# A second product with the scores in the quarters of a unit that have no experts' work, in a four-layer kernel on one Trainium2 core

## The reference, cut to what matters

```
for layer in 0, 1, 2, 3:
    xn = layernorm(x)
    x = x + attention(layer, xn) + feed_forward(layer, xn)
```

```
scores = q @ k.T * scale          # 512 x 512
p = softmax(scores)
o = p @ v
```

## Time and profile before

| what | value |
|---|---|
| median of 3 runs | 2046.42 us (2044.97 to 2046.79) |
| the profiled execution's own time | 2032.71 us |
| its span | 2030.9 us |
| its mean TensorE clock | 0.781 |
| TensorE busy | 1417.9 us (70%) |
| TensorE weight loads | 636.1 us (31%) |
| VectorE busy | 1310.7 us (65%) |
| ScalarE busy | 971.2 us (48%) |
| GpSimd busy | 290.0 us (14%) |

### The profile page before, as it was taken

One profiled execution on the slowest core, in us unless ns is written; L12 is line 12 of the kernel. 1 busy time (PEld: TensorE's weight loads), 2 busy tenths in 40 slices (PEclk: granted clock), 3 DMA queues, 4 the chain that ended last, 5 costly groups with the idle time before them and its releaser, 6 DMA issues.

```text
span 2030.9 us, 22370 instructions
## 1 busy us (share of the span) xinstructions
PE 1417.9 (70%) x6401; PEld 636.1 (31%) x6402; DVE 1310.7 (65%) x4041; ACT 971.2 (48%) x2237; POOL 290.0 (14%) x383
## 2 busy tenths in 40 slices
PE   6889799862244203641888998886877499899983
PEld 2445444431112101210355554221222133343331
DVE  5979889878888864761565665674565355455451
ACT  3889888834434441110455554443443244444441
POOL 0201010010000000266010011532013201000023
PEclk7989999985555555555998898676776799899995
DMA  3010001005000000221412232221102230111111
GB/s 109 24 47 25 40 30 37 1 11 191 1 0 1 0 1 23 72 77 44 107 57 75 75 102 62 62 39 50 36 28 49 84 113 21 25 56 44 40 31 49
DMA packets 151439, 98.41 MB, mean 48 GB/s; under 512 B 73328, under 2 KB 136117, under 8 KB 151265
## 3 DMA queue, kind: packets, MB, share of 16 engines
q1 hardware_dynamic: 145175, 84.40, 14.2%
q0 software_dynamic: 6144, 12.60, 2.2%
HBM read 60.83 MB, written 35.73 MB: 48 GB/s over the span
## 4 chain that ended last, share of the span: by engine, by line
PE 46%; DVE 30%; issue 8%; ACT 6%; another core or an unknown queue 6%; SPq 2%; DMA 2%; DVEq 0%
PE PS L465 38%; DVE RA L1560 5%; PE PS L461 4%; DVE RA L1562 4%; DVE nmx L1310 3%; DVE RA L1114 3%; DVE RA L1117 3%; PE PS L797 2%; SPq L2027 1%; PE PS L787 1%; DVE RB L1117 1%; DVE RB L1114 1%; DVE RA L1275 1%; DVE RA L1273 1%
## 5 line engine op out<-in xcount | busy, mean ns | idle before, releaser
L465 PE MATMUL PS<-RA 72*128 72x512 bf16 (+2 forms) x1360 | 483.9, 448 | 179.6 <-DVE nmx L1310 77.3
L1310 DVE TENSOR_REDUCE nmx<-PS 128x1 f32<-128x512 f32 x512 | 348.3, 686 | 333.6 <-PE PS L465 236.9
L1751 ACT ACTIVATE RA<-PS 128x512 f32<-128x512 f32 x512 | 302.8, 597 | 346.2 <-PE PS L465 274.0
L465 PEld LDWEIGHTS PS<-RA 72*128 72x128 bf16 (+3 forms) x1360 | 121.6, 105 | 495.8 <-issue 246.4
L465 PE MATMUL PS<-RA,Vs 128*32 128x512 f32 x1240 | 207.7, 667 | 3.6 <-ACT RA L1751 1.1
L1882 ACT ACTIVATE RA<-RA 128x8 f32<-128x8 f32 x511 | 107.5, 210 | 168.0 <-DVE RA L1560 167.1
L465 PE MATMUL PS<-RB,RA 128*128 (+2 forms) x672 | 155.6, 350 | 6.9 <-DVE RA L1290 6.7
L461 PE MATMUL PS<-ident,RB 128*128 128x128 f32 (+1 forms) x329 | 62.0, 333 | 137.3 <-DVE RB L1492 123.3
L1926 POOL DMA_INDIRECT RA<-yd,RA x96 | 92.1, 959 | 458.8 <-DMA yd<-RA 276.3
L465 PE MATMUL PS<-RB 128*128 (+3 forms) x280 | 110.8, 534 | 43.1 <-ACT RB L1856 28.7
L1273 DVE SCALAR_TENSOR_TENSOR RA<-RA,PS 128x256 f32<-128x256 f32 (+1 forms) x144 | 56.7, 394 | 117.7 <-ACT RA L1727 117.7
(11 more groups left out here) (301 smaller groups left out, 2013.0 us busy)
## 6 DMA issues: line engine op xcount, KB each, us to landing
RA<-scr SPq DMA_DIRECT2D x288, 96.0 KB
xd<-Otok SPq DMA_DIRECT2D x36, 256.0 KB, 3.2
RA<-xd SPq DMA_DIRECT2D x72, 128.0 KB, 2.2
scr<-parts SPq DMA_DIRECT2D x48, 128.0 KB
yd<-RB SPq DMA_DIRECT2D x48, 128.0 KB, 1.8
RB<-in_L_ffn_W SPq DMA_DIRECT2D x24, 256.0 KB
scr<-parts SPq DMA_DIRECT2D x64, 48.0 KB
yd<-RA SPq DMA_DIRECT2D x48, 64.0 KB, 1.5
```

Source lines behind the costliest of these rows:

```text
L465: return e.matmul(o, l, r, start=first, stop=last)
L1310: e.tensor_reduce(nmx[:, (g + lx) % 3, c:c + 1], bank[(6, 0)[i % 2]], AX.X, ALU.max, negate=True).then_inc(*ROWMAX.up(layer, n, i))
L1751: e.activation(PR[(k + 64 * lx) % 5][:, i, :], bank[(1, 5)[i % 2]], ACT.Exp).then_inc(*EXP.up(layer, k, i))
```

## The change

`first_expert` and `expert_until` give the units of a layer in which the plan has work for TensorE. In every other unit below 64, each quarter now ends with the same product of 72 rows that it began with, into bank 4 or bank 2. No semaphore is raised by it and nothing reads the result.

```diff
+    first_expert = {2: 14, 3: 27}
     plan = {2: spread(expert_steps(0), 14, 2.05), 3: spread(expert_steps(1), 27, 2.25)}
     assert not plan[2][1]
+    expert_until = {layer: 1 + max(n for (n, i), tasks in plan[layer][0].items() for t in tasks if t[0] == "down") for layer in (2, 3)}
...
             for task in plan[layer][0].get((n, i), ()):
                 expert_step(lx, task)
+            if n < 64 and not experts_at(layer, n):
+                bk = 4 if n < first_expert[layer] and at_ >= 0 else 2
+                claim(bk)
+                mm(bank[bk], stk[0:72, (n // 4) % 4, 0, n % 4, 128 * i:128 * i + 128], stk[0:72, (n // 4) % 4, 1, n % 4, :])
+
+        def experts_at(layer, n):
+            return first_expert[layer] <= n < expert_until[layer]
```

## The result

The changed kernel took 2082.04 us (median of 5 runs, 2068.01 to 2087.78) against 2046.79 us for the kernel before (2044.97 to 2050.41): ratio 1.0162, 95% interval 1.0129 to 1.0194, so 33 us slower (26 to 40). The forecast was +39. Its profiled execution took 2068.01 us, the shortest of the five, and is compared with the 2032.71 of before: +35.3.

The account below looks back on a forecast made before the run. TensorE and VectorE were taken as balanced per quarter at 1.2 GHz, 0.89 and 0.86 us. The terms 28 + 12 + 6 + 1 - 8 gave +39 us, forecast 2085 us, range 2040 to 2115.

Parts of the forecast that it names:

- The bound: Quarters at 1.2 GHz: both engines need the same time, 0.89 us on TensorE, 0.86 on VectorE; the change disturbs this.
- The price at 1.2 GHz: Each added product on TensorE costs 445 ns at 1.2 GHz, half of that, 0.22 us, at 2.4 GHz.
- The two long stretches: Layer 2's units 46 to 63 and layer 3's 0 to 26: TensorE 83% busy, clock 0.71 and 0.70; each 15 to 20 us longer.
- Non-value quarters: Long stretches, 120 quarters without values: some 74 cold ones pay 0.445 us each, less 15%, +28 us; warm ones pay nothing.
- Value quarters: Long stretches, 40 quarters with values, half cold: 13.3 us, the last one's hidden in a 3.23 us wait, +12 us.
- Units 0 to 13: Layer 2: hidden in units 0 to 5, then about 14 quarters at the cold price, +6 us; nothing in the scatter.
- The 22 us that I kept for the range: Layer 2's scatter: one more product of 2.7 us in some 8 quarters, if that spacing is per product; not in the sum.
- The banks: Bank 2 in units 56, 58 and 62 of layer 2: TensorE waits for copies, 0 to 3 us in all, none taken.
- Weight loads: All 240 added products: as many weight loads, with no separate term in the sum.
- No waking by 72 rows: Cold stretches: added 72-row products don't wake the clock, as ten score products end to end didn't at two places.
- What the clock gives back: Long stretches: three spared clock falls, each keeping two value quarters at 1.53 in place of 2.83 us, -8 us.
- The rule of the Trainium skill: Continuous matmuls get the fast clock; by it the faster rival's sum would hold, -20 us, 2026 us, chance 0.15.

Follow-up runs that it names:

- e2: Added 72-row product only in units 46 to 63 of layer 2 (72 of the 240), against the kernel before: ratio 1.0046, +9 us.
- e3: Added 72-row product only in units 0 to 26 of layer 3 (108 of the 240), against the kernel before: ratio 1.0058, +12 us.
- e12: Added 72-row product only in the value units (60 of the 240), against the kernel before: ratio 1.0029, +6 us.
- e1: Added 72-row product only in units 0 to 13 of layer 2 (56 of the 240), against the kernel before: ratio 1.0051, +10 us.
- e4: All 240 added products with 32 moving columns in place of 512, against the kernel before: ratio 1.0093, +19 us.
- e7: Added 72-row product made twice in each quarter, 480 in all, against the kernel before: ratio 1.0364.
- e8: Two added products of 128 rows (constant identity and ones) in each such quarter, against the kernel before: ratio 1.0021.
- e10: No added product; kernel's own second score product runs over 128 rows, rows 75 to 127 zero, against the kernel before: 0.9868, 2024.09 against 2048.44 us.
- e5: The changed kernel once more, one added 72-row product a quarter, against the kernel before on another chip: ratio 1.0130.

## Why the prediction was right, point by point

The time came as forecast, 33 us against 39, and so did the mechanism: TensorE's added streaming at 1.2 GHz, with no waking of the clock. The terms of the sum came less well. Two of them were about twice too large, one that gave time back isn't to be seen, and two small costs were missing; that these errors cancel to 6 us is luck.

- The bound. Right: TensorE and VectorE were level at 0.87 us a quarter at 1.2 GHz, and one more product made TensorE the later one, 1.28 us.
- The price at 1.2 GHz. Forecast 445 ns, measured 439, and 427 from start to start; at 2.4 GHz 0.22, measured 0.22 (1.75 less 1.53 us in a value quarter).
- The two long stretches together. Forecast 28 and 12, less the clock's 8, 32; e2 and e3 give 21 us with an interval from some 11 to 31.
- Non-value quarters, +28. The price was right, their number wasn't. The term had 74 cold quarters; in the changed kernel's trace 24 spacings of the maxima in layer 3's units 0 to 24 lie between 1.2 and 1.35 us (before 2) and 9 in layer 2's units 46 to 59 (before 0; 14 in e2). Some 31 to 36 quarters at 0.42 us are 13 to 15 us, an estimate. The term took the share of the time at the lower clock, 0.6, for a share of the quarters. But half of the time goes into a few long spacings: before, 19 of layer 3's 100 are over 2.5 us and take 82 of 170 us.
- Value quarters, +12: e12 gives 6, not distinguishable from 12 or 0. With the 13 to 15 above, 6 makes up the 21 of the stretches. Perhaps the wait behind the values hides more than the last quarter of four; that wasn't measured.
- Units 0 to 13, +6: e1 gives 10 (4 to 17). Units 0 to 5 hid the product as forecast, 1 us. Units 6 to 8 paid 3 us, and the rest, 5 to 7 in the profiles of e1 and of the changed kernel, lies in the units with the scatter, which I had put at nothing. The 22 us that I kept for the range there didn't come. The first two rows are from before, the others from the changed kernel, units 0 to 5 and 6 to 8 each:

```profile
817.00:858.00 41.00, 25.45 (x62) 10.43 (x63) 32.90 (x102) 2.88 (x6) 14.05 (x14) 0.50 0.20 63
858.00:879.00 21.00, 14.59 (x38) 4.63 (x36) 19.00 (x46) 8.50 (x15) 5.76 (x4) 0.50 0.16 48
818.00:860.00 42.00, 32.77 (x87) 12.54 (x88) 33.03 (x102) 2.88 (x6) 13.69 (x14) 0.54 0.20 59
860.00:884.00 24.00, 20.34 (x52) 7.67 (x51) 19.71 (x46) 8.62 (x15) 5.97 (x4) 0.50 0.16 48
```

- Layer 3's unit 27. It has no added product and no term, and takes 15.3 us in the changed kernel's profile and in e3's, 11.6 before. The clock is lower there (0.57 and 0.58, before 0.91). Why it stayed down wasn't looked for.
- The banks. I said 0 to 3 us for waits. No wait of note appears in the runs of products above; the claims' cost was not isolated, since e4 keeps them together with the weight loads.
- Weight loads. I priced them with the product and thought them free without it. In e4's dense run a claim, a weight load and a narrow product together cost 0.03 us, so the sum didn't suffer. Part of e4's +19 us stays unexplained.
- No waking by 72 rows. Right, and the strongest of the points: 6.15 us end to end at 0.50 here. In e7 the clock stayed at 0.50 for 75 us, from 1262 to 1337, with TensorE busy for 72.44 of them and values among the score products (the row stands below).
- What the clock gives back, -8. Not shown, and luck in one execution: in the profiled one layer 2's stretch kept 1.0 from 1311 to 1355, and that alone took back all that the stretch should have paid. But e2 at 0.70 paid 12 us for the same products, and e3's stretch at 0.68 was no faster in clock than before either. The clock goes with the spread of the runs of this kernel: over the five of the result, 2068.01 us at a mean of 0.787 and 2087.78 at 0.773. One reading of the earlier trace rows in the prediction is off: the fall at 1282 comes while TensorE still waits, not after the wait.
- The rule of the Trainium skill (page "TensorE: Matmul & The Clock Gate", section "Why this matters for your kernels"), to keep TensorE continuously busy with matmuls for the fast clock, fails in places of this kernel for products of 72 rows (e7, the row below) and mostly holds once half of the products have 128 (e8, a mean clock of 0.93). The row of e7 from 1262 to 1337 us:

```profile
1262.00:1337.00 75.00, 72.44 (x185) 24.98 (x184) 31.46 (x77) 23.12 (x43) 16.45 (x17) 0.50 0.12 21
```

## What to carry to other kernels

A filler product paid here only where it raised the clock, and whether it would could be read beforehand: look for a run of the same shape, end to end, and at the granted clock beside it. The product of 72 rows was a weak filler and made the time worse at 1.2 GHz, where it costs twice. Before adding work, see if the work at hand can be made fuller for nothing: 53 rows of zeros gave 1.3% here, the added product took 1.6%.

## What was not expected of the hardware

- The clock has memory: dense 72-row products did not raise it from 0.5 (6.15 us end to end), but it stayed at 1.0 with them once it was there (36 us in e7, 44 us in the changed kernel, values and transposes among them). Rows count: with 128 rows in half of the score products, part of them zeros, it rose (e10).
- Being busy doesn't always hold the clock. In the kernel before it fell just behind 1330 us, though TensorE had been busy without a gap. The products there were float32, half of them of 128 rows and half of a single one:

```profile
1327.00:1330.00 3.00, 3.00 (x16) 2.15 (x16) 2.48 (x3) 0.00 (x0) 0.00 (x0) 1.00 0.11 27
1330.00:1331.00 1.00, 1.00 (x4) 0.19 (x3) 0.63 (x3) 0.65 (x3) 0.00 (x0) 0.66 0.00 0
```

- Chips differ in the scatter. The units 9 to 13 of layer 2 take 96 us in the changed kernel's first profile and 25 in that of e5, the same kernel on another chip, where nothing stands still while GpSimd scatters. This is most of the 82 us between the two executions, and so probably of the difference between the two levels of the kernel before (2046 and 1951 us), of which no profile was taken on the second chip. Its cause was not looked for. The row of e5 for these units, against the second of the changed kernel's stages above:

```profile
885.00:910.00 25.00, 21.69 (x92) 6.05 (x92) 24.07 (x50) 11.03 (x20) 18.99 (x20) 0.79 0.29 94
```
